# Second normalisation in a token-routed transformer block: its mean from an extra column of the output projection, its squares summed on ScalarE

## The chip, the cores and the metric

One core of one Trainium2 chip. The metric is the device time of one execution in microseconds (us), the median of three. The core has a tensor engine (PE; its weight loads are shown apart, as PEld), VectorE (DVE), ScalarE (ACT), GpSimd (POOL) and SyncE (SP, which here only issues DMAs). The engines run programs of their own and meet at semaphores.

## What is computed

64 images of 3x96x96 become 36 patch tokens each, with a class token in front and 77 text tokens behind: 114 tokens of width 256 per image. One block follows:

```python
h = tokens                                    # (64, 114, 256)
h = h + attn(layernorm(h))                    # linear attention, 16 heads of 16
h = h + ffn(layernorm(h))                     # top-1 of 8 experts

# attn: Q, K = elu(x Wq + bq) + 1, elu(x Wk + bk) + 1; V = x Wv + bv
#       KV = sum_s K V;  Z = 1 / (Q . sum_s K + 1e-6);  out = (Q KV Z) Wo + bo
# ffn:  logits = x Wgate;  e = argmax;  r = sigmoid(max);  xs = x * r
#       out = (xs Wup[e] * silu(xs Wg[e])) Wdown[e]
# layernorm: (x - mean) / sqrt(var + 1e-5), no weights
```

## The kernel before, in words

The work has three stages. First (up to about 60 us) the patches are multiplied with the token weights, and weights are prepared. Each float32 product of this stage and of the next is made of three: operands are split into a high and a low part (line 964 makes the low ones), and `product` (lines 1344 to 1349) multiplies high by high, high by low and low by high.

Then comes the **pair loop**: 32 pairs of images, each with 2 x 114 tokens. It is a software pipeline. Each engine has a `step(i)` that calls its parts for pair i and for its neighbours, in an order written out by hand, and each engine executes its queue strictly in that order; a part that waits for a semaphore holds up all that stands behind it. On PE a step is (lines 1509 to 1529): `rank(i-4)`, `key_value(i-1)`, `turn_attention(i-2)`, `project(i)` (keys, gate, values), `project_out(i-2)`, `apply(i-1)`, `turn_tokens(i+1)`, `queries(i)`.

The output projection and the queries share one pair of PSUM banks, b_w, in turn. ScalarE puts the bias row into b_w (`seed_bias`), `project_out(p)` adds the attention output times Wo on top of it, VectorE reads it (`residual`, `gate_logits`), and `queries(p+2)` overwrites it; so it waits for `logits_ready` (line 1482). The projection is 264 columns wide: 256 of Wo, and 8 in which the gate weights are multiplied into Wo beforehand (`gate_columns`, line 1230), centred so that a mean cancels. The moving side of the query product is padded from 228 to the same 264 columns (`QW`, line 72).

What happens to a pair p after its output projection:

- VectorE, step p+2: `residual` (line 1080) adds b_w and the tokens into a row buffer, one instruction of 2 x 256 elements; `gate_logits` (1088) makes the logits of the gate; `attention` and `tokens_low` for other pairs; last in the step `stats_2` (1097): bn_stats and bn_aggr for each of the two images. Then the next step begins with `masked` (1057), which waits for `key_value`.
- GpSimd, step p+3: `rstd2_of` (613 to 630) makes 1/std, minus the mean, a copy of the mean for the row, and a ratio; `top_value` (638) scales the greatest logit. Between them stand `scatter` of pair p-1 and `rstd1_of` of pair p+5.
- ScalarE: `centred` (787 to 793) subtracts the mean from the rows in place, two instructions, behind `values` in step p+3; `tanh` (785) in step p+4 gives the sigmoid, and waits for `top_value`.
- VectorE `route` (1116) finds the expert, PE `rank` the place of each token among those of its expert, VectorE `places` (1147) puts it down.
- GpSimd, step p+4: `scatter` (649 to 665) completes the row (its elements 256 to 258: mean, gain, token id) and writes the rows of 260 elements to DRAM with two indirect DMAs, sorted by expert.

The third stage takes 64 tiles of 128 sorted rows in 32 **duos**: PE turns the rows (1632), multiplies with the gate and up weights (1608), ScalarE takes silu (933), VectorE multiplies (1266), PE turns and multiplies with the down weights (1619, 1644), VectorE adds the mean, the centred row and the product (1277), GpSimd scatters the result to the output (740). The second addend `rows + MEAN` restores the residual.

The change touches the border of stages two and three as well, where the queues are again written out by hand. ScalarE (lines 941 to 955):

```python
attention_high(PAIRS - 2); seed_bias(PAIRS - 2); S.activation(silu_ahead[:], ...)
tanh(PAIRS - 4); denominators(PAIRS - 1); centred(PAIRS - 3); tanh(PAIRS - 3)
attention_high(PAIRS - 1); straight(range(-2, 1), duo_step)
centred(PAIRS - 2); tanh(PAIRS - 2); duo_step(Turn(0, 1))
centred(PAIRS - 1); tanh(PAIRS - 1); straight(STEPS_B, duo_step)
```

(semicolons stand for line ends), and GpSimd, behind its `step(PAIRS)`, lines 724 to 732:

```python
count_chosen(PAIRS - 2); scatter(PAIRS - 3); count_chosen(PAIRS - 1)
rstd2_of(PAIRS - 2); top_value(PAIRS - 2); rstd2_of(PAIRS - 1)
scatter(PAIRS - 2); top_value(PAIRS - 1); scatter(PAIRS - 1)
```

In ScalarE's `duo_step(j)` the parts are, in order: the copy `actT` of duo j-1 (928), silu of duo j (933), the copy `xsT` of duo j+2 (939).

## Time and profile before

| | |
|---|---|
| median of 3 executions | 454.02 us (454.0 to 454.45) |
| the profiled execution | 453.9 us, span 452.1 us |
| mean granted PE clock | 0.981 of full speed |
| DMA | 46.36 MB, mean 103 GB/s |
| pair loop | about 60 to 321 us |
| border of the two stages | about 321 to 345 us |
| duos | about 334 to 441 us |

Busy tenths of each engine in 40 equal slices of the span, with the granted clock (9 is 90% or more):

```profile
PE   7999999999999999999999999999689999999990
PEld 7999899999999999999999999899677888888870
DVE  5669469999999999999999999997664434344440
ACT  5454466777777777777777777776525444444430
POOL 4055223877877877877877877776467756565662
PEclk9999999999999999999999999999889999999995
```

A slice is 11.3 us. The pair loop is slices 6 to 28, the border slices 29 to 31. "Releaser" in the rows below is the instruction whose semaphore ended a wait. PE instructions overlap, and the end of a matmul's bar is modelled, so the starts are what to compare. The span is first to last instruction; the execution's time is 1.8 us longer.

### The profile page before, as it was taken

Reading aid. Unit: us, or ns where it says so; the run is one execution under the profiler, and the core shown is the slowest. Engines: PE = TensorE matmul, PEld = TensorE weight load, DVE = VectorE, ACT = ScalarE, POOL = GpSimd, SP = SyncE. Lnnn points to the kernel's source line nnn. Section 1 sums busy time; section 2 is a strip of 40 time slices with the busy share of each in tenths; the row PEclk is TensorE's granted clock in tenths of the full one; section 3 lists DMA queues with packets and bytes.
Section 4 is the critical chain, followed back from the end, with each engine's and each line's share of the span. In section 5 each row is a group of like instructions: output and inputs, shape, how many; then the busy total and the mean of one; then the engine's idle time right before and its main releaser. Section 6 shows DMA issues by size and latency. Waiting matters only on the chain.

```text
span 452.1 us, 11750 instructions
## 1 busy us (share of the span) xinstructions
PE 428.8 (95%) x3685; PEld 406.9 (90%) x3685; DVE 330.2 (73%) x1115; ACT 278.6 (62%) x672; POOL 291.3 (64%) x662
## 2 busy tenths in 40 slices
PE   7999999999999999999999999999689999999990
PEld 7999899999999999999999999899677888888870
DVE  5669469999999999999999999997664434344440
ACT  5454466777777777777777777776525444444430
POOL 4055223877877877877877877776467756565662
PEclk9999999999999999999999999999889999999995
DMA  8973221323232121133121122068123982221120
GB/s 282 348 248 96 59 55 51 106 76 108 81 94 62 60 80 51 37 106 97 37 58 51 38 56 66 23 174 235 57 93 92 291 274 81 83 73 66 65 77 14
DMA packets 34143, 46.36 MB, mean 103 GB/s; under 512 B 8843, under 2 KB 25857, under 8 KB 34083
## 3 DMA queue, kind: packets, MB, share of 16 engines
q1 hardware_dynamic: 24860, 30.50, 22.6%
q0 software_dynamic: 9216, 15.12, 10.6%
q8 instruction: 30, 0.49, 0.5%
q14 instruction: 31, 0.25, 0.2%
q10 hardware_dynamic: 6, 0.00, 0.0%
HBM read 26.87 MB, written 17.17 MB: 97 GB/s over the span
## 4 chain that ended last, share of the span: by engine, by line
PE 86%; DVE 3%; issue 3%; POOL 2%; ACT 2%; DMA 1%; POOLq 0%; SPq 0%; DVEq 0%; ACTq 0%
PE b_kg L1608 11%; PE b_w L1347 7%; PE b_w L1348 6%; PE b_w L1349 6%; PE b_att L1462 6%; PE b_kg L1347 5%; PE b_kg L1349 4%; PE b_kg L1348 4%; PE b_att L1399 4%; PE b_t L1412 3%; PE b_v L1349 3%; PE b_v L1347 3%; PE b_v L1348 3%; PE b_att L1644 3%; PE b_w L1644 3%
## 5 line engine op out<-in xcount | busy, mean ns | idle before, releaser
L662 POOL DMA_INDIRECT sorted_rows<-rows,place x64 | 75.6, 1181 | 20.3 <-issue 9.7
L740 POOL DMA_INDIRECT out<-result,rows_all x64 | 62.4, 976 | 36.4 <-DVE result L1277 24.3
L1608 PE MATMUL b_kg<-wgu,xsT 128*128 x256 | 66.1, 381 | 0.1
L1266 DVE SCALAR_TENSOR_TENSOR act_u<-b_kg,rows_all,silu_g 128x128 f32<-128x128 f32 x64 | 19.5, 346 | 57.1 <-ACT silu_g L933 57.1
L846 ACT ACTIVATE q_exp<-b_w,bq_s 128x228 f32<-128x228 f32 x64 | 28.9, 452 | 32.4 <-PE b_w L1349 32.4
L1608 PEld LDWEIGHTS b_kg<-wgu,xsT 128*128 128x128 f32 x256 | 43.8, 190 | 3.8 <-issue 0.2
L1347 PE MATMUL b_w<-xnT_hi,wq_hi 128*128 128x264 f32 x128 | 39.2, 306 | 1.1 <-DVE logits L1088 1.0
L1347 PE MATMUL b_kg<-wkgv_hi,xnT_hi 128*114 128x264 f32 x128 | 38.7, 302 | 0.4 <-DVE patch_out L1005 0.4
L1462 PE MATMUL b_att<-kv_sb,qT 128*114 128x136 f32 x256 | 35.2, 281 | 1.9 <-issue 1.9
L1348 PE MATMUL b_kg<-wkgv_lo,xnT_hi 128*114 128x264 f32 x128 | 36.4, 284 | 0.0
L1349 PE MATMUL b_w<-xnT_hi,wq_lo 128*128 128x264 f32 x128 | 36.4, 284 | 0.0
L1348 PE MATMUL b_w<-xnT_lo,wq_hi 128*128 128x264 f32 x128 | 36.4, 284 | 0.0
L1349 PE MATMUL b_kg<-wkgv_hi,xnT_lo 128*114 128x264 f32 x128 | 36.4, 284 | 0.0
L1349 PE MATMUL b_v<-wkgv_hi,xnT_lo 128*114 128x256 f32 x128 | 36.0, 281 | 0.0
L1347 PE MATMUL b_v<-wkgv_hi,xnT_hi 128*114 128x256 f32 x128 | 36.0, 281 | 0.0
L1347 PE MATMUL b_w<-wo_hi,attnT_hi 128*114 128x264 f32 x124 | 35.8, 289 | 0.0
L1348 PE MATMUL b_w<-wo_lo,attnT_hi 128*114 128x264 f32 x124 | 35.8, 289 | 0.0
L1348 PE MATMUL b_v<-wkgv_lo,xnT_hi 128*114 128x256 f32 x128 | 35.7, 279 | 0.0
L1349 PE MATMUL b_w<-wo_hi,attnT_lo 128*114 128x264 f32 x124 | 35.6, 287 | 0.0
L801 ACT ACTIVATE xn<-rows_all,shift,rstd 114x255 f32<-114x255 f32 x64 | 34.8, 597 | 0.0
L1462 PEld LDWEIGHTS b_att<-kv_sb,qT 128*114 128x114 f32 x256 | 31.9, 179 | 2.1 <-issue 2.1
L933 ACT ACTIVATE silu_g<-b_kg,rows_all 128x128 f32<-128x128 f32 x64 | 20.1, 364 | 18.1 <-PE b_kg L1608 18.1
(225 smaller groups left out, 1450.7 us busy)
## 6 DMA issues: line engine op xcount, KB each, us to landing
rows_all<-sorted_rows SPq DMA_DIRECT2D x64, 130.0 KB, 2.9
rows_all<-in_x SPq DMA_DIRECT2D x18, 384.0 KB, 4.8
rows_all<-in_txt SPq DMA_DIRECT2D x32, 154.0 KB
wgu<-in_wgu_in SPq DMA_DIRECT2D x8, 256.0 KB, 3.0
rows_all<-patch_out SPq DMA_DIRECT2D x48, 36.0 KB
sorted_rows<-tail_rows SPq DMA_DIRECT2D x9, 130.0 KB, 2.1
sorted_rows<-rows,place POOLq DMA_INDIRECT x64, 3.7
wdown<-in_wdown_in SPq DMA_DIRECT2D x2, 512.0 KB, 4.5
```

The lines of the kernel that those rows point to most:

```text
L662: G.indirect_dma_start(out=scratch[0:EXPERTS * REGION, :], out_offset=bass.IndirectOffsetOnAxis(ap=place[:, k, b:b + 1], axis=0), in_=rows ...
L740: G.indirect_dma_start(out=out, out_offset=bass.IndirectOffsetOnAxis(ap=rows_all[:, t.n, ID:ID + 1].bitcast(I32), axis=0), in_=result[:, k ...
L801: last = S.activation(xn[:, b, 1:], rows_all[0:TOK, 2 * p + b, 1:D], ACT.Identity, bias=shift1[:, p % 8, b:b + 1], scale=rstd1[:, p % 8, b ...
L846: S.activation(q_exp[:, c, :], at, ACT.Exp, bias=bq_s[:, c:c + 1])
L933: last = S.activation(silu_g[:, t.slot(4)], b_gu[m.slot(2)][:, t.slot(2) * D:t.slot(2) * D + INNER], ACT.Silu, scale=rows_all[:, t.n, GAIN ...
L1266: last = V.scalar_tensor_tensor(act_u[:, t.slot(4)], b_gu[m.slot(2)][:, up:up + INNER], rows_all[:, t.n, GAIN:GAIN + 1], silu_g[:, t.slot( ...
L1347: T.matmul(to, left_hi, right_hi, start=start, stop=False, skip_group_check=seeded)
L1348: T.matmul(to, left_hi, right_lo, start=False, stop=False, skip_group_check=seeded)
L1349: return T.matmul(to, left_lo, right_hi, start=False, stop=stop, skip_group_check=seeded)
L1462: last = T.matmul(b_att[0:TOK, b, c * KVW:(c + 1) * KVW], qT[:, c, b * TOK:(b + 1) * TOK], kv_sb[:, b * KC + c].rearrange("p j w -> p (j w ...
L1608: last = T.matmul(to, xsT[:, t.slot(6), k, :], wgu[:, bass.ds(e, 1), k, :], start=(k == 0), stop=(k == KC - 1))
L1644: last = T.matmul(down_bank(m)[:, t.slot(2) * D:(t.slot(2) + 1) * D], actT[:, t.slot(6)], wdown[:, bass.ds(e, 1), :], start=True, stop=True)
```

## The change

Two columns are added to the output projection (264 to 266, line 72 and what follows). One gives the mean over the 256 columns of the attention output with its bias: gate_c gets a column of 1/256, and the preparation that folds the gate into Wo folds it in as well. The other is zero. With the mean of the tokens, known from the first normalisation and now kept for each pair (`neg1`), it gives minus the mean of the residual sum. So:

- VectorE's `residual` is a small instruction for minus the mean, a wait for it, and one instruction for each image that adds projection, minus the mean and tokens: the rows come out centred. `stats_2` and its four instructions go.
- ScalarE's `centred` goes. `square_sums` takes its place: two Square instructions, each with an accumulator output, for the variance. It waits for the rows alone, and in the step it stands ahead of `tanh` and `keys` (it stood behind `values`). In the border it stands where `centred` stood.
- GpSimd's `rstd2_of` starts from the sums of squares, has four instructions (five before), and stands in the step behind `scatter` and `rstd1_of` (ahead of both before).

The core of the diff (left out: renamed semaphores and buffers, KGW replaced by WOW in buffers, in the bias row and in the shapes of the host's arrays):

```diff
-QW = KGW
+GW = EXPERTS + 2
+WOW = D + GW
+QW = WOW
...
-        gate_mean, wo_gates, bo_gate = b_v[:, 0:EXPERTS], b_v[:, EXPERTS:3 * EXPERTS], b_v[0:BIAS_R, 3 * EXPERTS:4 * EXPERTS]
+        gate_mean, wo_gates, bo_gate = b_v[:, 0:EXPERTS], b_v[:, EXPERTS:EXPERTS + KC * GW], b_v[0:BIAS_R, EXPERTS + KC * GW:EXPERTS + 3 * GW]
...
-                G.tensor_scalar(ve1[:, 0, :], mv1[:, p % 2, :, 1], LN_EPS, None, ALU.add).then_inc(rstd1_step, 1)
-                G.tensor_scalar(ve1[:, 1, :], mv1[:, p % 2, :, 0], -1.0, None, ALU.mult).then_inc(rstd1_step, 1)
+                G.tensor_scalar(ve1[:], mv1[:, p % 2, :, 1], LN_EPS, None, ALU.add).then_inc(rstd1_step, 1)
+                G.tensor_scalar(neg1[:, k, :], mv1[:, p % 2, :, 0], -1.0, None, ALU.mult).then_inc(rstd1_step, 1)
...
             def rstd2_of(p):
 
                 k = p % 4
-                pool.wait_ge(mv2_ready, p + 1)
+                pool.wait_ge(squares_ready, p + 1)
                 if p >= 1:
-                    pool.wait_ge(rstd2_step, 5 * p)
+                    pool.wait_ge(rstd2_step, 4 * p)
                 if p >= 1:
                     pool.wait_ge(top_n_ready, p)
-                if p >= 4:
-                    pool.wait_ge(centred_ready, p - 3)
-                G.tensor_scalar(ve2[:], mv2[:, k, :, 1], LN_EPS, None, ALU.add).then_inc(rstd2_step, 1)
-                G.tensor_scalar(mean_neg[:, k, :], mv2[:, k, :, 0], -1.0, None, ALU.mult).then_inc(rstd2_step, 1)
-                pool.wait_ge(rstd2_step, 5 * p + 1)
+                G.tensor_scalar(ve2[:], square_sum[:, k, :], 1.0 / D, LN_EPS, ALU.mult, ALU.add).then_inc(rstd2_step, 1)
+                G.tensor_scalar(rows[:, k, :, MEAN], mean_neg[:, k, :], -1.0, None, ALU.mult).then_inc(rstd2_step, 1)
+                pool.wait_ge(rstd2_step, 4 * p + 1)
                 G.tensor_tensor(rstd2[:, k, :], ve2[:], half_neg[0:TOK, :], ALU.pow).then_inc(rstd2_step, 1)
-                pool.wait_ge(rstd2_step, 5 * p + 3)
-                G.tensor_copy(rows[:, k, :, MEAN], mv2[:, k, :, 0]).then_inc(rstd2_step, 1)
+                pool.wait_ge(rstd2_step, 4 * p + 3)
...
             def scatter(p):
...
                 pool.wait_ge(tanh_ready, p + 1)
-                pool.wait_ge(centred_ready, p + 1)
...
             def step(i):
-                if 0 <= i - 3:
-                    rstd2_of(i - 3)
                 if 0 <= i - 4:
                     scatter(i - 4)
                 if 0 <= i + 2 < PAIRS:
                     rstd1_of(i + 2)
                 if 0 <= i - 3:
+                    rstd2_of(i - 3)
                     top_value(i - 3)
                     count_chosen(i - 3)
...
-            def centred(p):
-
-                act.wait_ge(rstd2_step, 5 * p + 2)
+            def square_sums(p):
+
+                act.wait_ge(h2_ready, p + 1)
+                if p >= 4:
+                    act.wait_ge(rstd2_step, 4 * (p - 3))
                 for b in range(2):
-                    last = S.activation(rows[:, p % 4, b, 0:D], rows[:, p % 4, b, 0:D], ACT.Identity,
-                                        bias=mean_neg[:, p % 4, b:b + 1])
-                last.then_inc(centred_ready, 1)
+                    last = S.activation(squares[:, b, :], rows[:, p % 4, b, 0:D], ACT.Square, accum_out=square_sum[:, p % 4, b:b + 1])
+                last.then_inc(squares_ready, 1)
...
                     seed_bias(i - 2)
+                if 0 <= i - 3:
+                    square_sums(i - 3)
                 if 0 <= i - 4:
                     tanh(i - 4)
...
                     values(i)
-                if 0 <= i - 3:
-                    centred(i - 3)
...
-            centred(PAIRS - 3)
+            square_sums(PAIRS - 3)
             tanh(PAIRS - 3)
             attention_high(PAIRS - 1)
             straight(range(-2, 1), duo_step)
-            centred(PAIRS - 2)
+            square_sums(PAIRS - 2)
             tanh(PAIRS - 2)
             duo_step(Turn(0, 1))
-            centred(PAIRS - 1)
+            square_sums(PAIRS - 1)
             tanh(PAIRS - 1)
...
                 dve.wait_ge(wo_done, p + 1)
                 if p >= 4:
+                    dve.wait_ge(rstd2_step, 4 * (p - 3))
                     dve.wait_ge(scattered[p % 4], 32 * (p // 4))
-                V.tensor_tensor(rows[:, p % 4, :, 0:D], out_banks(p)[0:TOK, :, 0:D],
-                                rows_all[0:TOK, 2 * p:2 * p + 2, 0:D], ALU.add).then_inc(h2_ready, 1)
+                V.scalar_tensor_tensor(mean_neg[:, p % 4, :], out_banks(p)[0:TOK, :, KGW], -1.0, neg1[:, p % 8, :], ALU.mult, ALU.add
+                                       ).then_inc(mean_ready, 1)
+                dve.wait_ge(mean_ready, p + 1)
+                for b in range(2):
+                    last = V.scalar_tensor_tensor(rows[:, p % 4, b, 0:D], out_banks(p)[0:TOK, b, 0:D], mean_neg[:, p % 4, b:b + 1],
+                                                  rows_all[0:TOK, 2 * p + b, 0:D], ALU.add, ALU.add)
+                last.then_inc(h2_ready, 1)
...
-            def stats_2(p):
-
-                dve.wait_ge(h2_ready, p + 1)
-                if p >= 4:
-                    dve.wait_ge(rstd2_step, 5 * (p - 3))
-                stats(lambda b: rows[:, p % 4, b, 0:D], stats2, mv2[:, p % 4], stats2_done, mv2_ready, p)
...
                     tokens_low(i + 1)
-                if 0 <= i - 2:
-                    stats_2(i - 2)
...
             attention_low(PAIRS - 1)
-            stats_2(PAIRS - 2)
             residual(PAIRS - 1)
...
             late_count()
-            stats_2(PAIRS - 1)
             duo_step(Turn(0, 0))
...
                 for b in range(2):
-                    to = out_banks(p)[0:TOK, b, 0:KGW]
+                    to = out_banks(p)[0:TOK, b, 0:WOW]
```

## Rows read from the trace of the kernel before

**Rows 1.** The page: busy time, share of the span, instructions of each engine.

```profile
PE 428.8 (95%) x3685; PEld 406.9 (90%) x3685; DVE 330.2 (73%) x1115; ACT 278.6 (62%) x672; POOL 291.3 (64%) x662
```

**Rows 2.** The list of waits: engine, what, releaser: us, times, longest.

```profile
PEld b_w L1347 <- DVE logits L1088: 1.8, 3, 1.0
```

**Rows 3.** Timeline, PE, 200 to 210.5 and 308 to 345: start, us, what, [idle before].

```profile
202.10 0.28 PE L1349 MATMUL b_w<-wo_hi,attnT_lo 128*114 128x264 f32 x1
202.22 1.09 PE L1462 MATMUL b_att<-kv_sb,qT 128*114 128x136 f32 x8
...
314.41 0.28 PE L1349 MATMUL b_w<-wo_hi,attnT_lo 128*114 128x264 f32 x1
```

**Rows 4.** Timeline of PE's weight loads, near 203 and near 315.

```profile
203.44 0.19 PEld L1347 LDWEIGHTS b_w<-xnT_hi,wq_hi 128*128 128x128 f32 x1
...
315.74 0.19 PEld L1347 LDWEIGHTS b_w<-xnT_hi,wq_hi 128*128 128x128 f32 x1 [0.34 <-DVE logits L1088]
```

**Rows 5.** Timeline, VectorE (DVE), 200 to 210: one steady step.

```profile
201.43 0.17 DVE L1128 TENSOR_REDUCE first<-ranked 114x2 f32<-114x16 f32 x1
201.63 0.17 DVE L1133 TENSOR_TENSOR chosen<-ranked,first 114x16 bf16<-114x16 f32 x1
201.73 0.68 DVE L1073 SCALAR_TENSOR_TENSOR k_sb<-k_exp,b_kg 114x512 f32<-114x512 f32 x1
202.42 0.69 DVE L1080 TENSOR_TENSOR rows<-b_w,rows_all 114x512 f32<-114x512 f32 x1
203.03 0.35 DVE L1088 SCALAR_TENSOR_TENSOR logits<-b_w,rstd,gate_part 114x8 f32<-114x8 f32 x2
...
205.26 0.74 DVE L1018 BATCH_NORM_STATS2 stats<-rows 114x6 f32<-114x256 f32 x2
...
206.21 0.69 DVE L1057 TENSOR_TENSOR kv_sb<-b_att,con_s 128x544 f32<-128x544 f32 x1
```

**Rows 6.** Timeline, VectorE, near 340: the two result sums of one duo.

```profile
340.33 0.86 DVE L1277 SCALAR_TENSOR_TENSOR result<-rows_all,b_w 128x256 f32<-128x256 f32 x2
```

**Rows 7.** Timeline, ScalarE (ACT), 200 to 210: two neighbouring k_exp.

```profile
199.62 0.70 ACT L813 ACTIVATE k_exp<-b_kg,one_neg 114x512 f32<-114x512 f32 x1
...
208.06 0.69 ACT L813 ACTIVATE k_exp<-b_kg,one_neg 114x512 f32<-114x512 f32 x1
```

**Rows 8.** Timeline, GpSimd (POOL), 308 to 350: the end of the pair loop.

```profile
318.15 0.23 POOL L623 TENSOR_SCALAR ve<-mv 114x2 f32<-114x2 f32 x1 [1.93 <-DVE mv L1022]
...
319.60 0.19 POOL L630 TENSOR_TENSOR ratio<-spread,rstd 114x2 f32<-114x2 f32 x1
...
326.06 0.20 POOL L638 TENSOR_TENSOR top_n<-top,ratio 114x2 f32<-114x2 f32 x1
...
338.40 0.19 POOL L654 TENSOR_SCALAR route_w<-tanh_top 114x2 f32<-114x2 f32 x1 [0.56 <-ACT tanh_top L785]
...
342.24 0.20 POOL L638 TENSOR_TENSOR top_n<-top,ratio 114x2 f32<-114x2 f32 x1
```

**Rows 9.** Timeline, ScalarE, 308 to 350: the end of the pair loop.

```profile
326.40 0.52 ACT L767 CAST attnT_hi<-b_att 128x456 fp32r<-128x456 f32 x1
...
337.30 0.92 ACT L791 ACTIVATE rows<-rows,mean_neg 114x256 f32<-114x256 f32 x2
```

**Rows 10.** Timeline, VectorE, 308 to 350: the end of the pair loop.

```profile
327.63 0.62 DVE L964 TENSOR_TENSOR attnT_lo<-b_att,attnT_hi 128x456 fp32r<-128x456 f32 x1
```

**Rows 11.** Timeline, PE, 308 to 345: the end of the pair loop.

```profile
321.52 1.49 PE L1462 MATMUL b_att<-kv_sb,qT 128*114 128x136 f32 x8 [1.88 <-issue]
...
328.40 0.19 PE L1380 MATMUL b_att<-chosen,earlier 114*114 114x16 bf16 x1 [1.65 <-DVE attnT_lo L964]
...
343.08 1.13 PE L1644 MATMUL b_att<-wdown,actT 128*128 x4 [0.80 <-ACT actT L928]
```

**Rows 12.** Busy time by stretch: us, each engine (x instructions), PEclk, DMA, GB/s.

```profile
320.00:335.00 15.00, 10.48 (x65) 9.73 (x66) 9.17 (x48) 5.09 (x12) 7.51 (x19) 0.77 0.13 33
```

**Rows 13.** Groups by line: the load of a function table.

```profile
L943 ACT ACT_TABLE_LOAD x1 | 1.3, 1283 | 0.0
```

More of the change, by code:

```diff
@@ L168, in build @@
         mv1 = sb("mv1", [TOK, 2, 2, 2])
-        ve1 = sb("ve1", [TOK, 2, 2])
+        ve1 = sb("ve1", [TOK, 2])
+        neg1 = sb("neg1", [TOK, 8, 2])
         rstd1 = sb("rstd1", [TOK, 8, 2])
@@ L218, in build @@
             rows = sb("rows", [TOK, 4, 2, ROW], at=room)
-            stats2 = sb("stats2", [TOK, 2, 6], at=room)
-            mv2 = sb("mv2", [TOK, 4, 2, 2], at=room)
+            squares = sb("squares", [TOK, 2, D], at=room)
+            square_sum = sb("square_sum", [TOK, 4, 2], at=room)
             ve2 = sb("ve2", [TOK, 2], at=room)
@@ L607, in rstd1_of @@
                 pool.wait_ge(rstd1_step, 5 * p + 2)
-                G.tensor_tensor(rstd1[:, k, :], ve1[:, 0, :], half_neg[0:TOK, :], ALU.pow).then_inc(rstd1_step, 1)
+                G.tensor_tensor(rstd1[:, k, :], ve1[:], half_neg[0:TOK, :], ALU.pow).then_inc(rstd1_step, 1)
                 pool.wait_ge(rstd1_step, 5 * p + 3)
-                G.tensor_tensor(shift1[:, k, :], ve1[:, 1, :], rstd1[:, k, :], ALU.mult).then_inc(rstd1_step, 1)
-                G.tensor_tensor(spread1[:, k, :], ve1[:, 0, :], rstd1[:, k, :], ALU.mult).then_inc(rstd1_step, 1)
+                G.tensor_tensor(shift1[:, k, :], neg1[:, k, :], rstd1[:, k, :], ALU.mult).then_inc(rstd1_step, 1)
@@ L613, in rstd2_of @@
+                G.tensor_tensor(spread1[:, k, :], ve1[:], rstd1[:, k, :], ALU.mult).then_inc(rstd1_step, 1)
             def rstd2_of(p):
                 k = p % 4
-                pool.wait_ge(mv2_ready, p + 1)
+                pool.wait_ge(squares_ready, p + 1)
                 if p >= 1:
-                    pool.wait_ge(rstd2_step, 5 * p)
+                    pool.wait_ge(rstd2_step, 4 * p)
                 if p >= 1:
                     pool.wait_ge(top_n_ready, p)
-                if p >= 4:
-                    pool.wait_ge(centred_ready, p - 3)
@@ L771, in bias_row @@
                 act.wait_ge(bias_row_done, 1)
-                S.copy(bias_rows[:], b_w[0:TOK, 0, 0:KGW]).then_inc(bias_row_ready, 1)
+                S.copy(bias_rows[:], b_w[0:TOK, 0, 0:WOW]).then_inc(bias_row_ready, 1)
             def seed_bias(p):
@@ L777, in seed_bias @@
                 act.wait_ge(q_parts, p + 2)
-                S.copy(b_w[0:TOK, :, 0:KGW], bias_rows[:].rearrange("p (b w) -> p b w", b=1).to_broadcast([TOK, 2, KGW])).then_inc(bias_seeded, 1)
+                S.copy(b_w[0:TOK, :, 0:WOW], bias_rows[:].rearrange("p (b w) -> p b w", b=1).to_broadcast([TOK, 2, WOW])).then_inc(bias_seeded, 1)
             def tanh(p):
@@ L1545, in gate_weights @@
                         at = k * D + c * P
-                        T.matmul(wo_gates[:, c * EXPERTS:(c + 1) * EXPERTS], wo_rows_s[:, at:at + P], gate_c[:, k, :],
+                        T.matmul(wo_gates[:, c * GW:(c + 1) * GW], wo_rows_s[:, at:at + P], gate_c[:, k, :],
                                  start=(k == 0), stop=(k == KC - 1))
@@ L1585, in _ @@
             pe.wait_ge(bias_step, 12)
-            T.matmul(b_w[0:TOK, 0, 0:KGW], ones_bf[:], bias_bf[:], start=True, stop=True).then_inc(bias_row_done, 1)
+            T.matmul(b_w[0:TOK, 0, 0:WOW], ones_bf[:], bias_bf[:], start=True, stop=True).then_inc(bias_row_done, 1)
             pe.wait_ge(patches_ready, PT)
@@ L1756, in biases @@
 def biases(bo):
-    s = zeros(1, KGW)
+    s = zeros(1, WOW)
     s[0, 0:D] = bo
```

29 lines of the change are left out of this document (15 added, 14 removed).

## The prediction

> **What bounds the kernel now.** I read the page's table of engines first: the tensor engine (PE) is busy for 95% of the span, VectorE for 73%, ScalarE and GpSimd for less [rows 1]. So work taken off VectorE or ScalarE is worth something only where PE waits for it. The list of waits names one such place in the pair loop: the weight loads of the query product (line 1347 into b_w) waited 1.8 us in three waits for the gate logits of line 1088 [rows 2]. That looks like nothing for 32 pairs, so I went to the timeline of one steady step, first PE, then its weight loads, then VectorE.
>
> On PE the last matmul of the output projection starts at 202.10 and its bar ends at 202.38. Behind it come the eight apply matmuls [rows 3], the four transposes of the next pair's tokens, and the query product. The query product overwrites b_w, so its first weight load waits for the logits. It starts at 203.44; in the step near 315, where no transposes stand before it, the same load starts at 315.74 and is marked as having waited for the logits [rows 4]. On VectorE the residual sum starts at 202.42, 0.04 us behind the last projection matmul, issues for 0.61 us, and the two logit instructions end at 203.38 [rows 5]. So the load comes 0.06 us behind the logits, and 1.34 us behind the start of the last projection matmul. In the step near 315 the logits open it 1.33 us behind the start of the same matmul, at 314.41 [rows 3]. The difference, 0.01 us, is all the slack the steady step has. PE's apply and transposes happen to last exactly as long as VectorE's residual and logits, and the wait does not show. The steady steps are alike in this; in a few late ones VectorE comes late by itself, and those are the visible waits. **The loop is therefore bound by PE and by the chain PE, residual, logits, PE alike.** What lengthens that chain is paid once a step, in full; what leaves VectorE elsewhere is nearly free.
>
> **The change part by part.**
>
> *Residual.* One instruction over 512 elements becomes a two-element one (the negated mean), a wait of VectorE for its own result, and two of 256 elements with a pointer scalar. For the small one with its wait I take 0.20 us, the distance between two dependent small instructions at 201.43 and 201.63 [rows 5]; the ends are 0.16 and 0.25. For the two halves the nearest rows are the result sums, same instruction, same kinds of operands, 0.86 us for two [rows 6], of which the next instruction overlaps 0.08 as behind the residual now: 0.78. For them the ends are 0.67 (no price for the pointer) and 0.86. Together 0.98 against 0.61. I take +0.40 on the chain with the longer reach of the semaphore, ends +0.22 and +0.50; less the slack, 0.39 a step. The logits wait stands before the query products of pairs 2 to 31, thirty times. The two late steps with a visible wait (1.46 of the 1.8 us [rows 2]; the third is the one near 315 [rows 4]) get some relief from the lighter VectorE, so I take half there, 0.2. Sum: 28 x 0.39 + 2 x 0.2 = **11.3 us**, ends 6.3 and 15. The Trainium skill, VectorE: DVE Perf Modes, the section on the TRN2 errata, gives a PSUM source 120 cycles plus one per element at 0.96 GHz; that would make 0.25 us of the two added instructions, and 28 x 0.24 = 7 us of this term (471.5 in all).
>
> *Statistics.* Two bn_stats and two bn_aggr leave the end of VectorE's step: 205.26 to 206.21, 0.95 us [rows 5]. Nothing on PE waits for them, and the instruction behind them waits for PE's key-value product anyway; 0, ends -0.5 and 0 for the whole loop beyond what the late steps got.
>
> *Columns.* The output projection and the padded query product go from 264 to 266 columns: 24 matmuls a pair, 768 in all. Neighbours start 0.12 us apart [rows 3], 0.45 ns a column: 768 x 2 x 0.45 ns = 0.7, taken as **0.8 us**, ends 0.6 and 1.
>
> *ScalarE.* Centring (0.92 us for two [rows 9]) goes, two squares with accumulator outputs come, for which no row exists: 0.8 to 1.4 us for the two, taken as 1.0. They move ahead of tanh and the keys, so k_exp comes 1 us later in its step. It ended at 200.32 and VectorE took it up at 201.73 [rows 5, 7]: 1.4 us of cover, so 0; beyond 1.4 it would be paid. The normalised rows, the values and the denominators follow k_exp and end as they did, since the centring is no longer behind them.
>
> *GpSimd in the loop.* One instruction fewer, and rstd2 moves behind the scatter and rstd1. A turn is then about 7.5 us (a scatter with its two DMAs up to 3.8, rstd1 and rstd2 some 1.6 each, two small ones [rows 8]) in a step that lasts 8.44 us now, from one k_exp to the next [rows 7], and 8.8 then; so the tanh that waits for it is not late. 0, ends 0 and 1 us in all.
>
> *The end of the loop*, where queues written out by hand meet, is the second cost.
> (1) GpSimd now does scatter(28), rstd2(29), top_value(29) where rstd2(29) used to stand first and was done at 319.79 (from 318.15, 1.64 us, 1.5 without the copy). So top_value(29) starts 1.5 us after 326.06 [rows 8]. ScalarE's tanh(29) waits for it, and behind tanh in its queue stands attention_high(31), whose end was at 326.92 [rows 9] and comes at 328.4. VectorE's attention_low(31), taken up at 327.63 [rows 10], can't start before that, and PE's rank, at 328.40 now [rows 11], waits for it: **+0.8 us**.
> (2) The last residual, **+0.4 us**, before rank(31).
> (3) The squares of pair 30 stand in ScalarE's queue where its centring stood, at 337.30 [rows 9], behind the first silu. Its statistics used to be long done; now rstd2(30), top_value(30) and tanh(30) follow only after the squares, 1.9 us later, with the copy of actT(0) behind them.
> (4) For pair 31 it is worse. The squares stand behind duo_step 1, rstd2(31) waits for them, and in GpSimd's queue scatter(30) stands behind rstd2(31) and top_value(31) behind scatter(30). From scatter(30)'s first instruction to top_value(31) it is 3.84 us (338.40 to 342.24) [rows 8]. ScalarE can't go on to actT(1) before tanh(31). My timetable, with 1.2 us from (1) and (2): squares(30) end 339.4, tanh(30) 341.2, PE's down(0) 341.7, rows turned 343.0, xsT 343.8, squares(31) end 344.7, rstd2(31) 346.2, scatter(30), top_value(31) 350.0, tanh(31) 350.3, actT(1) ready 350.8. PE's second down product, at 343.08 now [rows 11], comes at 350.9. The whole of (1) to (4) is **+7.8 us**, ends 6 and 10.
>
> *Clock.* PE then idles 5 to 6 us. Behind today's idle time of 1.88 us eight apply matmuls take 1.49 us instead of 1.09 [rows 3, 11], and the granted clock of that stretch is 0.77 [rows 12], so part of it is at 1.2 GHz. Some microseconds at the lower level cost **+2.0 us**, ends 0 and 4.
>
> **Sum.** The profiled execution took 453.9 us (span 452.1), 0.1 under the median of 454.02. 453.9 + 11.3 + 0.8 + 7.8 + 2.0 = **475.8 us**. The ends of the terms together give 467 to 484.
>
> **The rivals.**
> - *The chain is not what opens the query product* and PE has slack of its own, so that only columns, tail and clock are paid: 453.9 + 0.8 + 7.8 + 2 = 464.5. For it: the list shows three waits only. Against it: the 0.01 us above, in every step.
> - *The tail is covered*, by work I placed wrongly, and only (1) and (2) cost: 453.9 + 11.3 + 0.8 + 1.2 = 467.2. For it: a hand-made timetable of four queues errs easily. Against: every link is a wait in program order.
> - *Not slower: the relief of VectorE decides.* Place: the late steps, where VectorE reaches the residual late and PE waits. Price: at most the 1.46 us of [rows 2], less 0.8 for columns, 453.2. It decides if the new chain from the last projection matmul to the logits is no longer than today's 0.96 us and the tail is covered too. Against: three instructions in place of one.
> - *Squares cost a table switch.* A load of a function table takes 1283 ns [rows 13]; two of them a pair before the keys (2.6 us, over the 1.4 of cover) would add 2 us or more to each step, 530 us and up. The Trainium skill, ScalarE: Activation LUTs, the section on table sets, says that cheap functions "appear in *every* set as filler", without naming the square there, and puts a switch at about 2.7 us; by that filler rule there is none. Nothing in this trace shows a square.
> - *The change does nothing that counts*, chain and tail both hidden: 454.7.
>
> **How the numbers follow.** Forecast 0.70; only the tail 0.07; only the chain 0.12; relief 0.05 (0.03 over the bound, 0.02 within); table 0.04; nothing 0.02. A measurement of this kernel can tell 0.2%, 0.9 us, from no change. Faster 0.03, same 0.04, slower 0.93. The range takes in the ends of the forecast and the two partial cases: 464 to 484.
>
> **What would show it.** In a steady step: residual to logits 0.4 us longer, a wait of PE for the logits of about 0.4 us in all thirty steps, a step of 8.8 to 8.9 us. ScalarE's k_exp about 1 us later in the step, VectorE's k_sb not moved. Near the end: ScalarE idle before tanh(30) and, for over 5 us, before tanh(31), with PE idle at the second down product and a lower clock behind it. The forecast is wrong if the logits end no later, or if the copy of actT(1) isn't behind tanh(31).

## The result, and the profile after

The changed kernel takes 477.18 us (median, 476.3 to 478.57), 1.051 times the kernel before (95% interval 1.0477 to 1.0543): 5% slower, 1.4 us beyond the forecast of 475.8. The profiled execution took 476.93 us with a span of 475.1, 23.0 more than before. These are the page's lines that answer to the table and to [rows 1]:

```profile
PE 440.6 (93%) x3685; PEld 412.2 (87%) x3685; DVE 313.4 (66%) x1053; ACT 275.2 (58%) x736; POOL 276.8 (58%) x630
...
PE   7999999999999999999999999998765999999990
PEld 7999899999999999999999999898654888888870
DVE  5668567878878878878878878876443344344440
ACT  5444567667667667667667667665422444444440
POOL 3155222776776776776776775674526756556563
PEclk9999999999999999999999999999788999999996
```

VectorE lost 16.8 us of work and ScalarE 3.4, and neither shows in the time. PE is busy 12 us more, 8.3 of them in the 29 steps (246.5 us before, 254.9 after): there the bar of the token transposes used to overlap that of the query product behind it and no longer does, and the columns come on top. It idles more as well. The place of the new idle time is in the list of waits (engine, what, releaser: us in total, times, longest):

```profile
DVE kv_sb L1057 <- PE b_att L1394: 34.1, 32, 1.6
...
PEld b_w L1342 <- DVE logits L1094: 11.8, 30, 1.4
...
ACT tanh_top L782 <- POOL top_n L637: 10.6, 3, 5.3
...
POOL ve L623 <- ACT squares L790: 9.5, 2, 5.8
...
PE b_att L1639 <- ACT actT L926: 6.0, 2, 5.4
```

The first line is VectorE's relief: 34.1 us, 1.1 us a step, spent waiting for PE's key-value product. The second is what [rows 2] was: three waits and 1.8 us have become thirty waits and 11.8 us. The last three are the chain at the end of the pair loop.

One steady step, near 209 (compare [rows 3, 4, 5]). The changed kernel's timeline of PE (start, us, engine, line, operation; in brackets a wait and its releaser):

```profile
209.47 0.29 PE L1344 MATMUL b_w<-wo_hi,attnT_lo 128*114 128x266 f32 x1
...
211.19 0.39 PE L1342 MATMUL b_w<-xnT_hi,wq_hi 128*128 128x266 f32 x1
```

The timeline of PE's weight loads, the one of the query product:

```profile
211.18 0.19 PEld L1342 LDWEIGHTS b_w<-xnT_hi,wq_hi 128*128 128x128 f32 x1 [0.33 <-DVE logits L1094]
```

VectorE's timeline, from k_sb to the logits:

```profile
208.99 0.68 DVE L1073 SCALAR_TENSOR_TENSOR k_sb<-k_exp,b_kg 114x512 f32<-114x512 f32 x1
209.79 0.16 DVE L1081 SCALAR_TENSOR_TENSOR mean_neg<-b_w,neg 114x2 f32<-114x2 f32 x1
209.99 0.87 DVE L1085 SCALAR_TENSOR_TENSOR rows<-b_w,mean_neg,rows_all 114x256 f32<-114x256 f32 x2
210.78 0.35 DVE L1094 SCALAR_TENSOR_TENSOR logits<-b_w,rstd,gate_part 114x8 f32<-114x8 f32 x2
```

The small instruction starts 0.32 us behind the start of the last projection matmul, where the residual started before. The halves start 0.20 later, the logits 0.79 after that, 0.99 us in all against 0.61. The logits end at 211.13 and the weight load starts at 211.18, 1.71 us behind the projection's last start against 1.34. So each step is 0.37 us longer by the chain. Between projections lie 8.88 us against 8.46, and the missing 0.05 us are columns.

Where the 23.0 us went, by the starts of three matmuls: the last of pair 0's output projection (66.88 before, 67.40 after), the last of pair 29's (314.41, 327.05), and the second down product (343.08, 364.75):

| | before | after | more |
|---|---|---|---|
| to the end of pair 0's projection | 66.9 | 67.4 | 0.5 |
| 29 steps of the pair loop | 247.5 | 259.65 | 12.1 |
| end of the loop, to the second down product | 28.7 | 37.7 | 9.0 |
| the rest of the span | 109.0 | 110.35 | 1.3 |

The end of the loop (compare [rows 8, 9, 11]). ScalarE's timeline, both tanh and, between them, the end of the last squares:

```profile
355.20 0.20 ACT L782 ACTIVATE tanh_top<-top_n 114x2 f32<-114x2 f32 x1 [2.16 <-POOL top_n L637]
...
358.61 0.19 ACT L790 ACTIVATION_READ_ACCUMULATOR squares<-rows 114x1 f32 x1
364.14 0.20 ACT L782 ACTIVATE tanh_top<-top_n 114x2 f32<-114x2 f32 x1 [5.34 <-POOL top_n L637]
```

GpSimd's timeline, from rstd2(31) to top_value(31):

```profile
358.89 0.19 POOL L623 TENSOR_SCALAR ve<-square_sum 114x2 f32<-114x2 f32 x1 [3.72 <-ACT squares L790]
...
361.22 1.24 POOL L660 DMA_INDIRECT sorted_rows<-rows,place  x1 [0.32 <-POOL place L657]
...
363.91 0.20 POOL L637 TENSOR_TENSOR top_n<-top,ratio 114x2 f32<-114x2 f32 x1
```

PE's timeline, from pair 29's projection over the first gate product (L1603) to the two down products (L1639):

```profile
327.05 0.29 PE L1344 MATMUL b_w<-wo_hi,attnT_lo 128*114 128x266 f32 x1
...
342.48 0.19 PE L1375 MATMUL b_att<-chosen,earlier 114*114 114x16 bf16 x1 [1.55 <-DVE attnT_lo L962]
...
347.70 3.39 PE L1603 MATMUL b_kg<-wgu,xsT 128*128 x8
...
355.81 1.13 PE L1639 MATMUL b_w<-wdown,actT 128*128 x4 [1.96 <-ACT actT L926]
...
364.75 2.07 PE L1639 MATMUL b_att<-wdown,actT 128*128 x4 [5.43 <-ACT actT L926]
```

The first gate product in the trace of the kernel before:

```profile
334.29 1.99 PE L1608 MATMUL b_kg<-wgu,xsT 128*128 x8
```

ScalarE waits 2.16 us before tanh(30) and 5.34 us before tanh(31). GpSimd starts rstd2(31) at 358.89, when the squares end, then does the scatter of pair 30, and only at 363.91 top_value(31). PE waits 1.96 and 5.43 us for the copies behind the two tanh. Behind the last projection it runs at its lower level in two places: the eight matmuls at 347.70 take 3.39 us against 1.99, and the down product at 364.75, behind the 5.43 us, takes 2.07 instead of 1.13. The down product at 355.81, behind 1.96 us, takes 1.13. The experiments show that the second place goes with the long wait, and that the first can't be put down to the change. The granted clock of the stretches (columns as in [rows 12]):

```profile
60.00:200.00 140.00, 138.25 (x1326) 133.29 (x1325) 112.28 (x397) 98.96 (x282) 86.66 (x245) 1.00 0.24 69
...
340.00:350.00 10.00, 6.40 (x43) 5.42 (x42) 5.38 (x37) 1.70 (x4) 4.23 (x12) 0.84 0.16 46
...
365.00:370.00 5.00, 5.00 (x21) 4.18 (x22) 1.48 (x4) 1.38 (x5) 3.78 (x5) 0.74 0.28 84
```

### The profile page after: what moved, and what is told of

The parts are those of the page before. It is cut to its first block and busy times, and to the rows that moved or that the text cites. A ratio compares the mean times of both kernels' runs of the same rounds, so it can differ in the third digit from the quotient of the medians.

```text
span 475.1 us, 11693 instructions
## 1 busy us (share of the span) xinstructions
PE 440.6 (93%) x3685; PEld 412.2 (87%) x3685; DVE 313.4 (66%) x1053; ACT 275.2 (58%) x736; POOL 276.8 (58%) x630
## 5 line engine op out<-in xcount | busy, mean ns | idle before, releaser
L1603 PE MATMUL b_kg<-wgu,xsT 128*128 x256 | 67.6, 388 | 0.0
L1603 PEld LDWEIGHTS b_kg<-wgu,xsT 128*128 128x128 f32 x256 | 45.0, 195 | 4.0
L1057 DVE TENSOR_TENSOR kv_sb<-b_att,con_s 128x544 f32<-128x544 f32 x32 | 23.2, 724 | 34.1 <-PE b_att L1394 34.1
L1342 PE MATMUL b_w<-xnT_hi,wq_hi 128*128 128x266 f32 x128 | 40.0, 313 | 5.3 <-DVE logits L1094 2.4
L1344 PE MATMUL b_w<-xnT_hi,wq_lo 128*128 128x266 f32 x128 | 36.6, 286 | 0.0
L1343 PE MATMUL b_w<-xnT_lo,wq_hi 128*128 128x266 f32 x128 | 36.6, 286 | 0.0
L1343 PE MATMUL b_w<-wo_lo,attnT_hi 128*114 128x266 f32 x124 | 36.3, 292 | 0.0
L1342 PE MATMUL b_w<-wo_hi,attnT_hi 128*114 128x266 f32 x124 | 36.2, 292 | 0.0
L1344 PE MATMUL b_w<-wo_hi,attnT_lo 128*114 128x266 f32 x124 | 36.1, 291 | 0.0
L652 POOL TENSOR_SCALAR route_w<-tanh_top 114x2 f32<-114x2 f32 x32 | 6.5, 203 | 50.2 <-ACT tanh_top L782 50.2
```

The costliest lines, as they stand in the source:

```text
L1057: V.tensor_tensor(kv_sb[:], b_kv.rearrange("p a (j w) -> p a j w", j=1).to_broadcast([P, 2 * KC, 2, KVH]), mask.rearrange("p (a j w) -> p ...
L1342: T.matmul(to, left_hi, right_hi, start=start, stop=False, skip_group_check=seeded)
L1343: T.matmul(to, left_hi, right_lo, start=False, stop=False, skip_group_check=seeded)
L1344: return T.matmul(to, left_lo, right_hi, start=False, stop=stop, skip_group_check=seeded)
L1603: last = T.matmul(to, xsT[:, t.slot(6), k, :], wgu[:, bass.ds(e, 1), k, :], start=(k == 0), stop=(k == KC - 1))
```

## The experiments

Each was timed in alternation with the kernel before; ratios are to it, with their 95% intervals. "Step" is the distance between the last matmuls of two neighbouring output projections.

**The border's order alone.** The changed kernel, with ScalarE's squares of the last two pairs earlier:

```diff
-            straight(range(-2, 1), duo_step)
-            square_sums(PAIRS - 2)
-            tanh(PAIRS - 2)
-            duo_step(Turn(0, 1))
-            square_sums(PAIRS - 1)
-            tanh(PAIRS - 1)
+            duo_step(Turn(0, -2))
+            square_sums(PAIRS - 2)
+            duo_step(Turn(0, -1))
+            square_sums(PAIRS - 1)
+            duo_step(Turn(0, 0))
+            tanh(PAIRS - 2)
+            duo_step(Turn(0, 1))
+            tanh(PAIRS - 1)
```

> The changed kernel, but at the end of the pair loop ScalarE does the squares of pairs 30 and 31 ahead of duo steps -1 and 0 instead of behind 0 and 1 (and the buffer of squares gets two more slots). Theory (the squares, rstd2, scatter(30), top_value(31), tanh(31) stand in a chain of queues): ScalarE no longer waits over 5 us before tanh(31), PE's second down product comes 8 us earlier counted from the last steady projection (30 instead of 37.7 us), and 1 us of lowered clock goes: 468.2 us, 9 us under the changed kernel. Rival (the tail is held by something else, the last scatters or the lowered clock): under 3 us are won, 474 or more.

Measured: 468.98 us, ratio 1.0344 (1.0307 to 1.0382), 8 us under the changed kernel. ScalarE's timeline shows both squares done early and both tanh without a wait:

```profile
341.36 0.43 ACT L790 ACTIVATE squares<-rows 114x256 f32<-114x256 f32 x1
...
345.11 0.42 ACT L790 ACTIVATE squares<-rows 114x256 f32<-114x256 f32 x1
...
352.27 0.21 ACT L782 ACTIVATE tanh_top<-top_n 114x2 f32<-114x2 f32 x1
...
356.56 0.21 ACT L782 ACTIVATE tanh_top<-top_n 114x2 f32<-114x2 f32 x1
```

PE's second down product comes 31.4 us behind the last matmul of pair 29's projection (326.44 to 357.83), against 37.7 in the changed kernel and 28.7 before. The step is 8.88 us as in the changed kernel. So the place of the squares of two pairs in one queue was worth 6.3 us up to there. From the second down product on the span has 108.9 us left, as before the change, against 110.35 in the changed kernel: another 1.4.

**The long residual alone**, put into the kernel before, which keeps its statistics, its centring, its 264 columns and GpSimd's order:

```diff
-                V.tensor_tensor(rows[:, p % 4, :, 0:D], out_banks(p)[0:TOK, :, 0:D],
-                                rows_all[0:TOK, 2 * p:2 * p + 2, 0:D], ALU.add).then_inc(h2_ready, 1)
+                V.scalar_tensor_tensor(nought[:, p % 4, :], out_banks(p)[0:TOK, :, KGW - 1], 0.0, nought2[:], ALU.mult, ALU.add
+                                       ).then_inc(mean_ready, 1)
+                dve.wait_ge(mean_ready, p + 1)
+                for b in range(2):
+                    last = V.scalar_tensor_tensor(rows[:, p % 4, b, 0:D], out_banks(p)[0:TOK, b, 0:D], nought[:, p % 4, b:b + 1],
+                                                  rows_all[0:TOK, 2 * p + b, 0:D], ALU.add, ALU.add)
+                last.then_inc(h2_ready, 1)
```

> The kernel before, with the long residual alone: a small instruction (zero, read from b_w), a wait for it, and two sums with that pointer scalar; statistics, centring, columns and GpSimd's order are as before. Theory (PE, residual, logits, PE is a chain without slack): a wait of PE for the logits of about 0.35 us in each of thirty steps, the step 0.37 us longer, 454.2 + 11 + 0.8 at the end = 466 us; VectorE is more loaded than in either kernel, so it may be late at k_sb, up to 470. Rival (the added columns, squares and GpSimd's order make the step longer, not the residual): 456 or less.

Measured: 466.86 us, ratio 1.0287 (1.0252 to 1.0321). The list of waits has the same line as the changed kernel, in a kernel that differs from the one before in nothing but these instructions:

```profile
PEld b_w L1356 <- DVE logits L1097: 11.8, 30, 1.4
```

The step is 8.83 us, 0.37 more than before. VectorE was not late at k_sb. The end of the loop is longer too, 31.9 us against 28.7, where 0.8 had been expected: PE gets to the rank of the last pair 1.6 us later (20.84 us behind pair 29's projection for 19.25), and the first gate product takes 3.65 us for 1.99. So not all that the changed kernel lost there comes from the squares.

**The short residual in the changed kernel.** One sum over 512 elements, the mean behind it without a wait; the squares take the mean as bias, and the centring is back on ScalarE (those parts are left out here):

```diff
+                V.tensor_tensor(rows[:, p % 4, :, 0:D], out_banks(p)[0:TOK, :, 0:D],
+                                rows_all[0:TOK, 2 * p:2 * p + 2, 0:D], ALU.add).then_inc(h2_ready, 1)
                 V.scalar_tensor_tensor(mean_neg[:, p % 4, :], out_banks(p)[0:TOK, :, KGW], -1.0, neg1[:, p % 8, :], ALU.mult, ALU.add
                                        ).then_inc(mean_ready, 1)
-                dve.wait_ge(mean_ready, p + 1)
-                for b in range(2):
-                    last = V.scalar_tensor_tensor(rows[:, p % 4, b, 0:D], out_banks(p)[0:TOK, b, 0:D], mean_neg[:, p % 4, b:b + 1],
-                                                  rows_all[0:TOK, 2 * p + b, 0:D], ALU.add, ALU.add)
-                last.then_inc(h2_ready, 1)
```

> The changed kernel with the short residual: one sum over 512 elements, the mean by one small instruction behind it without a wait, squares with the mean as bias on ScalarE, and the centring back on ScalarE behind the values (two instructions more than in the changed kernel). Theory: the chain is 0.08 us longer than in the kernel before instead of 0.37, so 0.29 us a step or 8.7 us are won; the border's chain stays and has the centring in it besides (0.8 us twice): 477.2 - 8.7 + 1 = 469.5 us. Rival (ScalarE's new work and GpSimd's order cost the steps): 477 or more, since ScalarE has more to do.

Measured: 468.26 us, ratio 1.0328 (1.0291 to 1.0365). ScalarE does 0.9 us a step more than in the changed kernel, and yet the step is 8.57 us, 0.31 less. The query's weight load stands 1.40 us behind the projection's last start, 0.06 more than before. The waits at the end of the loop are still there, ScalarE's 7.9 us for the 10.6 of the changed kernel, PE's 6.2 for 6.0, and that for the logits is back to three waits:

```profile
ACT tanh_top L784 <- POOL top_n L638: 7.9, 3, 4.5
...
PE b_att L1652 <- ACT actT L939: 6.2, 2, 5.6
...
PEld b_w L1355 <- DVE logits L1107: 1.9, 3, 1.0
```

**Columns alone.** `QW = KGW + 16` in the kernel before.

> The kernel before with the padded query product 16 columns wider (280 for 264), nothing else. Theory (each added column costs PE 0.46 ns and nothing hides it): 384 matmuls x 16 x 0.46 ns = 2.8 us, 457.0 us; the change's two columns in 768 matmuls are then 0.7 us. Rival (the weight load of 0.12 us sets the distance of matmuls, columns are free): 454.2.

Measured: 457.51 us, ratio 1.0077 (1.0049 to 1.0105); the step 8.54 us, 0.08 for 192 added columns, 0.42 ns each. Over 32 pairs that is 2.5 us; the other 1 us lies behind the loop. PE gets to the last pair's rank no later than before (18.9 us behind pair 29's projection for 19.25), but the first gate product takes 1.6 us longer:

```profile
336.70 3.58 PE L1608 MATMUL b_kg<-wgu,xsT 128*128 x8 [0.17 <-issue]
```

e10_moved below, which has no added column, shows nearly the same (3.43), so this 1 us is not shown to be columns. In the loop columns of the query product cost what the expectation said, no more.

**The statistics back on VectorE**, in the changed kernel, into buffers that nobody reads:

```diff
                     tokens_low(i + 1)
+                if 0 <= i - 2:
+                    stats_2(i - 2)
```

> The changed kernel with the two bn_stats and two bn_aggr back at the end of VectorE's step, into buffers that nobody reads. Theory (what left VectorE was worth nothing: its next instruction waits about 1.1 us a step for PE's key-value product): 477.2 us within 0.7, the step still 8.88 us. Rival (the relief of 0.95 us a step is worth part of itself, so the change's true cost was larger): 480 us or more.

Measured: 478.58 us, ratio 1.0534 (1.0496 to 1.0572), its profiled execution 476.62. The step is 8.88 us, and VectorE's wait for the key-value product has gone from 34.1 us to almost nothing:

```profile
DVE kv_sb L1060 <- PE b_att L1409: 2.9, 5, 0.9
```

The 30 us of VectorE that the change took away can be put back without a change of the step. The median is 1.4 us higher than the changed kernel's, more than the 0.7 that the theory allowed, with an interval that overlaps, and the profiled execution is 0.3 us shorter. The theory holds for the step; a cost or gain of a microsecond in all is not excluded.

**GpSimd's order alone.** The changed kernel, with `rstd2_of(i - 3)` first in GpSimd's step as before the change.

> The changed kernel with rstd2 of the last pair but three again first in GpSimd's step, ahead of scatter and rstd1. The prediction charged this move with 0.8 us, at the last pair's attention_low behind tanh(29). Theory now (VectorE's own queue, lengthened by the longer residual and by the lower clock of the output projection, gets there at the same moment, so the move costs nothing): 477.2 us within 0.5, and attention_low(31) starts no earlier counted from the last steady projection. Rival (the prediction's step): rank(30) 0.8 us earlier, 476.4.

Measured: 483.07 us, ratio 1.06 (1.0554 to 1.0647): slower than the changed kernel by 6 us in the medians and by 4 in the ratios (one of the four executions took 479.48). Both expectations missed. In the loop the step is 8.88 us as expected. At its end, GpSimd's timeline, from rstd2(29) to top_value(29):

```profile
338.62 0.19 POOL L623 TENSOR_SCALAR ve<-square_sum 114x2 f32<-114x2 f32 x1 [7.71 <-ACT squares L791]
...
343.69 0.20 POOL L637 TENSOR_TENSOR top_n<-top,ratio 114x2 f32<-114x2 f32 x1
```

and PE's, attention of the last pair and the first gate product:

```profile
345.36 0.23 PE L1376 MATMUL b_att<-chosen,earlier 114*114 114x16 bf16 x1 [3.81 <-DVE attnT_lo L963]
...
352.21 3.78 PE L1604 MATMUL b_kg<-wgu,xsT 128*128 x8
```

GpSimd waits 7.71 us for the squares of pair 29, with scatter(28) behind them, though tanh(28) is long done. So top_value(29), tanh(29), attention_high(31) and the rank on PE come late: the rank waits 3.81 us against 1.55, and PE then runs at its lower level up to the first gate product (3.78 us). The move that I had charged with 0.8 us saves 4 to 6 once the squares are on ScalarE.

**Folding the mean into the residual.** If the chain is the cost, the mean may come from a column and yet be free. The mean column goes first behind Wo, GpSimd writes the tokens' mean into element 257 of their row, and one sum over 2 x 257 elements gives both; with it the orders that the experiments above suggest:

```diff
+                G.tensor_copy(rows_all[0:TOK, 2 * p:2 * p + 2, D], mv1[:, p % 2, :, 0])
...
+                V.tensor_tensor(rows[:, p % 4, :, 0:D + 1], out_banks(p)[0:TOK, :, 0:D + 1],
+                                rows_all[0:TOK, 2 * p:2 * p + 2, 0:D + 1], ALU.add).then_inc(h2_ready, 1)
```

> Another way to the same sums, with a short chain: the mean column stands first behind Wo, the tokens' mean is written into the 257th element of their row by GpSimd, so one sum over 2 x 257 elements gives rows and mean together; minus the mean at the end of VectorE's step; squares (with the mean as bias) and centring both on ScalarE; the query product back at 264 columns; the border order of e1_border; top_value(31) ahead of scatter(30); and VectorE's table of early slots moved from the middle of steps 28 and 29 to the ends of steps 28 to 30, where it now idles. Theory (only the chain and the border cost): step 8.47 us, the two late steps' 1.4 us gone, 0.3 us for columns, 0.8 us won at PE's wait for actT(1): 454.0 - 1.9 = 452.1 us. Rival (squares, centring and columns have a cost of their own in the step): 455 or more.

Measured: 454.86 us, ratio 1.0014 (0.9989 to 1.0039). This kernel leaves something out: its query product is 264 columns wide and its projection 266, so expert 7's logit lacks a constant, and its time stands for the same work only because e11_folded, whose product is 266 wide, takes as long. The step is 8.50 us, 0.04 more than before, as much as its wider projection takes longer; of the waits for the logits one of 0.3 us is left in the list, and none in the late steps (8.50 and 8.51 us for 9.48 and 8.96). That is 1.4 us won in the late steps, and it went for columns (29 x 0.04) and the end of the loop (29.0 us against 28.7).

> e9_folded with the query product padded to 266 columns again, as in the change: in e9_folded it wrote 264 columns of b_w, so the last gate column of the output projection was overwritten instead of added to its seeded bias, and expert 7's logit lacked a constant; its time is to be read as that of the same work. Theory: the step grows from 8.50 to 8.52 us, everything else as in e9_folded: 454.5 us, no different from the kernel before, since what the late steps give (1.4 us) goes for columns (30 x 0.05) and the border. Rival (columns of the query product are dear, 0.05 us a step each side): 456 or more.

Measured, with `QW = WOW`: 455.32 us, ratio 1.0017 (0.9994 to 1.004), step 8.52. The change's sums, done without the longer chain, come out at the time before, with the moves of the order included; what the moves are worth alone is the next experiment. (The Trainium skill, PSUM — Partial Sum Buffer, the section on the four PSUM rules, says that ScalarE's writes don't set the bits by which a matmul adds or overwrites; by it the padding of the query product is what lets the seeded columns be added to. No time here bears on that.)

**The moves without the change.** The kernel before, with VectorE's table of early slots at the ends of steps 28 to 30 instead of in front of attention_low in steps 28 and 29, and

```diff
             rstd2_of(PAIRS - 1)
-            scatter(PAIRS - 2)
             top_value(PAIRS - 1)
+            scatter(PAIRS - 2)
```

> The kernel before with only the two moves of e9_folded that don't need its relief: the table of early slots at the ends of steps 28 to 30, and top_value(31) ahead of scatter(30). Theory: behind the statistics VectorE has no idle time at the end of its step, so the slots push the mask and all behind it, and the late steps stay; only the 0.8 us before actT(1) is won: 453.2 us. Rival (the moves alone are worth all that e9_folded wins): 452 us.

Measured: 452.52 us, ratio 0.9952 (0.9929 to 0.9975), the fastest so far with its twin below. I was wrong on where: the late steps shrank to 8.45 and 8.68 us (29 steps: 246.15 us, 1.4 less), though VectorE has its statistics. PE no longer waits for actT(1), but the end of the loop is not shorter (29.1 us), because the first gate product takes 1.4 us longer than in the trace of the kernel before:

```profile
332.28 3.43 PE L1613 MATMUL b_kg<-wgu,xsT 128*128 x8
```

Against this kernel the folded mean, which has the same moves in it, costs 2.3 us (e9_folded) and 2.8 (e11_folded), with intervals that don't touch: 0.05 us a step of it is columns, the rest is spread and was not taken apart.

**Two more moves at the end of the loop**: VectorE's `queries(PAIRS - 1)` ahead of `attention_low(PAIRS - 2)`, and PE's `load_experts(0)` behind `duo_step(Turn(0, -2))`.

> e10_moved, and two moves at the end of the pair loop that the waits of every trace so far point to: VectorE does the queries of the last pair ahead of attention_low(30), so that PE's apply(31) doesn't wait 1.9 us for them, and PE loads the first sixteen expert numbers behind duo step -2, where it waits anyway, instead of ahead of turn_attention(30), where it stops for 0.8 us. Theory: 1.5 and 0.8 us less on the path to the last projection, and a shorter stay at the lower clock: 452.5 - 2.3 - 0.5 = 449.7 us. Rival (the end of the loop is held by ScalarE's queue of seed, table load, tanh and denominators, and the time comes back at PE's wait for attention_low(31)): 452 us or more.

Measured: 452.87 us, ratio 0.9945 (0.9914 to 0.9975), no different from e10_moved. The profiled execution took 457.23 us, with a granted clock of 0.95 in the pair loop, so what its trace says of times is a hint and no more. PE's timeline:

```profile
326.75 0.19 PE L1385 MATMUL b_att<-chosen,earlier 114*114 114x16 bf16 x1 [2.65 <-DVE attnT_lo L964]
...
332.15 3.78 PE L1613 MATMUL b_kg<-wgu,xsT 128*128 x8
```

Pair 30's projection ends 7.8 us behind pair 29's (314.23 to 322.05) instead of 10.8. Of these 3 us PE gives 1.0 back at once, waiting 2.65 us for attention_low(31) against 1.65. From pair 29's projection to rank(31) it is 17.2 us, against 19.25 before and 18.8 in e10_moved. Then the first gate product runs at the lower level, 3.78 us against 1.99 before; but e10_moved has 3.43 there, so that doesn't explain why the 1.6 us between the two are missing from the median. That stays open.

## Why the prediction was right, and where its terms were off

The forecast was 21.9 us more, the profiled executions differ by 23.0: 0.5 up to pair 0's projection (not forecast), 10.7 by the chain in 29 steps and 1.4 by the columns (11.3 and 0.8 forecast for the whole loop), 9.0 at its end and 1.3 behind it (7.8, and 2.0 for the clock). Both mechanisms were the ones forecast; that the total came within 1.4 us is in part luck, since the misses of the terms have both signs and partly cancel.

*The chain.* Forecast: 0.39 us a step, thirty waits, 11.3 us. Measured: 0.37 us, thirty waits in the list; by e2_chain it is the residual's instructions alone. The small instruction and its wait took 0.20, as the rows of two dependent small ones had said, the halves 0.79 for 0.78. The Trainium skill's figure of 120 cycles for a PSUM source (VectorE: DVE Perf Modes, the section on the TRN2 errata) would have given 0.25 us for what measured 0.38; the rows of this kernel were the better source. That the late steps would get half of their share back was wrong: the query's load stands 2.77 and 2.15 us behind the projection in them, against 2.37 and 1.84, so they pay 0.40 and 0.31.

*The relief of VectorE.* Forecast 0, measured 0 in the step, and within about a microsecond in all: e5_stats.

*Columns.* Forecast 0.8 us, measured 1.3 to 1.4 (0.046 us a step, which is what the chain leaves of the step's 0.42). In e4_cols a column of the query product costs 0.42 ns; the output projection is dearer, see below. The step of the sum that took one price for both was mis-sized.

*ScalarE.* Forecast: the squares 1.0 us for two, no cost. Measured: the first starts at 206.40 and tanh behind the second at 207.21, 0.81 us, and no table load came in the loop. The rival of a table switch falls. As forecast, k_exp starts 0.8 us later in its step (6.78 us behind the last projection matmul for 5.96), and k_sb doesn't move.

*GpSimd's order.* Step (1), +0.8 us, failed in its reason. In the changed kernel VectorE takes attention_low(31) up at 341.71, straight behind its own routing of pair 30; ScalarE's copy for it ended at 341.59. Both came late together: VectorE through the longer residual (0.4) and pair 30's projection, which ended 11.9 us behind pair 29's for 10.8: 0.4 of that is the chain in the step before, 0.6 that the eight apply matmuls took 2.13 us for 1.49. In e4_cols and e10_moved, without chain or GpSimd's move, they take 2.13 too. So the size of this step was luck. And the order that I would have put back costs 4 to 6 us.

*The last two pairs.* Steps (3) and (4): 7.8 us with (1) and (2), measured 9.0 from pair 29's projection to the second down product, with 0.4 of the chain in it. The timetable had PE at the first down product at 341.7 and at the second at 350.9, 9.2 us apart; they are 8.9 apart. PE's wait for the second actT was forecast as 5 to 6 us and is 5.43 (the first, for which the prediction has no figure, is 1.96). Up to the last pair's rank, which is what (1) and (2) were to cost 1.2 us for, it is 20.03 us for 19.25, 0.8 more. The first gate product has 1.4, and the remaining 6.8 are (3) and (4), forecast as 6.6. e1_border shows that they are the squares' place: it takes 6.3 us away and leaves 2.7, in which its first gate product, 3.78 us, has 1.8.

*Clock.* Forecast 2.0, as what 5 to 6 us without work cost PE. That cost is shown: in the four kernels whose PE waits 5.4 to 5.6 us for actT(1) (the changed one, e3_short, e5_stats, e6_order) the down product behind it takes 2.07 us, in all others 1.03 to 1.15, and in the changed kernel the rest of the span is 1.3 us longer, 0.9 of it there. The 1.4 us of the first gate product are counted in the end of the loop above, and that they belong to the change is not shown: e4_cols (3.58) and e10_moved (3.43), with neither the longer residual nor the squares, have them too. With them the lower level comes to 2.7 us, without them to 1.3; both lie inside the stated ends.

*The range.* The ends of the terms, GpSimd's 1 us and the statistics' 0.5 included, add up to 466.3 and 484.9, not 467 and 484; nothing hangs on it.

The rivals: "the chain isn't what opens the query product" falls by e2_chain and e3_short, "the tail is covered" by e1_border, "relief decides" by e5_stats. No run has e1_border's order with the short residual and nothing else. e11_folded is the nearest and comes back to the time before, 1.0017, but with moves in it that alone win 0.5% (e10_moved).

## What to carry to other kernels

An engine without waits is not proof that nothing else binds: measure from the releaser's end to the start of what it releases, in every step; if that is the bare latency of a semaphore (0.05 to 0.06 us here), the two paths are equal and the shorter-looking one can't bear an instruction more. Before work is moved to an idle engine, write down for the first and last rounds what will then stand behind what in each queue; the steady loop here forgave a late result, the hand-over between the two loops didn't. And when a trade gives back less than it promised, look whether the freed engine simply waits at its next semaphore. Before a microsecond between two single traces is put down to an edit, look whether a kernel without the edit shows it too.

## What the runs showed of the hardware that I had not expected

Two columns more on the output projection cost more than columns of the query product. Twelve matmuls of 264 columns start over 1.33 us in the kernel before (313.08 to 314.41), twelve of 266 over 1.37 in the changed one (325.68 to 327.05), 3.6 ns a matmul for two columns; in e4_cols sixteen columns cost 6.7 ns a matmul. In e9_folded, where only the projection is wider, the step is 0.04 us longer; widening the query product as well (e11_folded) adds 0.02, which is also more than its 24 columns would cost at the 0.42 ns of e4_cols (0.01). Why is open; two columns and sixteen are the only steps in width that were run.

The lower level of the clock comes and goes at the end of the loop, whatever the edit. In nine of the twelve traces the first gate product takes 3.4 to 3.8 us, in e9_folded 2.65, and in e11_folded and the kernel before 1.99. Waits don't sort these: in front of the last two ranks PE waits 2.9 us in the kernel before and 2.8 in e4_cols and e10_moved, which have 3.58 and 3.43. In the changed kernel the granted clock stayed at 1.00 in the pair loop, where the weight loads of the query product waited 0.4 us a step and 1.4 at most. The 0.95 of e12_border's pair loop, with PE busy 70.00 of 70.00 us from 60 to 130, came without any idle time; no run here tells where it came from.
